# Graph attention on one core: VectorE's operands moved from SBUF to PSUM, part of the one-hot work of the last turns moved to VectorE, and the last stage reordered

## The chip, the cores and the metric

The kernel runs on one core of one Trainium2 chip. What counts is the device time of one execution in microseconds. The engines are written as in the profile: PE is TensorE, DVE is VectorE, ACT is ScalarE, POOL is GpSimd, and SP is the queue that issues most plain DMAs.

## The reference, cut to what matters

One layer of graph attention with 6250 nodes and 206250 edges that are sorted by their target node (6250 of them are loops from a node to itself), 8 heads of 16 columns, and a residual:

```python
h = relu(layernorm(x))
xm = h @ W_n2m.T; xl = xm @ Wl.T + bl; xr = xm @ Wr.T + br
e = ea_f @ We.T                       # ea_f: edge attributes, and their mean per node for a loop
u = leaky_relu(xl[src_f] + xr[dst_f] + e, 0.2)
logits = einsum('ehd,hd->eh', u, att)
mx = segment_max(logits, dst_f); p = exp(logits - mx[dst_f])
alpha = p / segment_sum(p, dst_f)[dst_f]
out = segment_sum(xl[src_f] * alpha, dst_f) + bias
return x + out @ W_m2n.T
```

`leaky_relu(z, 0.2)` is the larger of z and 0.2 z, which is also 0.2 z + relu(0.8 z).

## The kernel before

There are three stages: a prologue (to about 119 us of the trace), the edge loop (to about 2261 us), and the finale.

**Prologue.** It computes xl for all nodes into a table in HBM (`xl_table`), xr into SBUF, and the tables and masks that drive the loop.

**Edge loop.** The edges are cut in 806 pieces of 256, and 427 steps (`STEPS`) take two pieces each. POOL does nothing in this stage but gather the rows of xl for the pieces: 1612 indirect DMAs of 128 rows (line 807; L813 is its wait for the last landings), whose descriptors it writes itself, into a ring `xl_g` of 64 pieces. The engines run their lists in order of turns k, and in one turn they work on different steps. PE makes z of step k in a PSUM bank (`z_ps`, two banks): xr by a one-hot matrix (L828), the attributes (L832), and the transposed copy `xl_z` of the gathered rows (L836). ACT copies the gathered rows to `xl_z` (L906) two turns ahead, and before that waits until the gathers of that step have been issued and landed. ACT then copies z from PSUM to `uT` in SBUF (L939), and DVE makes the leaky relu of `uT` in place (L1027), with both of its inputs in SBUF. PE turns u into logits (L868) and 17 turns later (`LAG`) adds the weighted messages by a one-hot matrix (L882, with `onehot` made by ACT at L928 and L933 and `msg` made by DVE at L1018 and L1023); DVE adds the sums to `acc` (L983, L1006). Once in 8 steps (`BATCH`) come the pieces that find running maxima: two scans over 256 columns (L1037, L1043) into `forth` and `run_max`, a matmul that takes their ends (L849), two scans on one partition (L1051, L1054), then L1067, L1071, L1075 and L1076 on DVE, and transposes (L892, L893). The loop is rolled with a body of 48 turns; turns before 31 and behind the last round are written out. Past the last step (k from 427 on) 19 turns are left in which only the late work is done.

**Finale.** It walks 49 windows of nodes in 7 groups of 7 (b is a group). DVE adds xl to z of the loop edges (L1365), ACT makes the relu part (L1268), DVE joins both (L1370), multiplies, reduces, and finds the falls; ACT makes `weights` by Exp (L1272); DVE makes totals, shares, `old` (L1356) and `own` (L1358); PE transposes and adds them (L1220, L1222) and multiplies by the output matrix (L1235), ACT copies the result (L1294), and POOL adds it to `out` by an accumulating DMA (L1177). `xl_in` (two buffers) is loaded by SP once `own` of an earlier group is done, and `means` (L1318) is made a group ahead in the same loop.

## Time and profile before

| what | value |
|---|---|
| median of 3 runs | 2349.64 us (2345.63 to 2352.04) |
| the profiled execution | 2349.71 us |
| its span, first to last instruction | 2347.9 us |
| outside the span | 1.8 us |
| mean granted TensorE clock | 0.956 of full speed |

The span is what the trace shows, with all its times counted from its first instruction. Busy times of an engine are those of its instructions; an instruction that waits at the head of its engine's queue isn't counted.

### The profile page before, as it was taken

How to read it: one execution, taken by the hardware profiler on the slowest of the kernel's cores; microseconds unless marked ns; L12 is line 12 of the kernel's file. 1: busy time of each engine (PE TensorE's matmuls, PEld its weight loads, DVE VectorE, ACT ScalarE, POOL GpSimd, SP SyncE). 2: the span in 40 equal slices, each digit the busy share in tenths (PEclk: the TensorE clock that was granted, in tenths of full speed). 3: DMA queues.
4: the chain of work that ended last, by engine and by line, in shares of the span. 5: the costliest groups of instructions: out<-in, count | busy, mean ns of one | idle time of the engine just before them, and what ended most of it. 6: DMA issues, size and time to landing. Idle time of an engine off the chain costs nothing. (4 is left out here: it accounts for less than half of the span.)

```text
span 2347.9 us, 62160 instructions
## 1 busy us (share of the span) xinstructions
PE 2203.8 (94%) x11747; PEld 1371.5 (58%) x11748; DVE 1439.1 (61%) x4181; ACT 1550.3 (66%) x4329; POOL 1664.9 (71%) x1813
## 2 busy tenths in 40 slices
PE   3968999999999999999999999999999999999966
PEld 2723566655666566556656665666566656666655
DVE  5723566665666566656666666665666656666677
ACT  2613677676776677667767776777677767777753
POOL 3877777777777777777777777777777777777201
PEclk9956999999999999999999999999999999999989
DMA  5233444444444444444444444444444444444218
GB/s 170 78 86 89 114 116 122 112 110 115 122 115 114 116 119 117 114 116 116 117 114 118 113 118 114 117 114 116 114 121 112 116 112 120 113 116 114 57 54 135
DMA packets 317116, 263.56 MB, mean 112 GB/s; under 512 B 173619, under 2 KB 289637, under 8 KB 316438
## 3 DMA queue, kind: packets, MB, share of 16 engines
q1 hardware_dynamic: 254222, 142.33, 23.8%
q0 software_dynamic: 57632, 113.02, 20.8%
q10 hardware_dynamic: 4840, 3.68, 0.5%
q8 instruction: 131, 2.15, 0.4%
q14 instruction: 291, 2.38, 0.4%
HBM read 247.39 MB, written 16.89 MB: 113 GB/s over the span
## 5 line engine op out<-in xcount | busy, mean ns | idle before, releaser
L807 POOL DMA_INDIRECT xl_g<-xl_table,src_tab x1612 | 1581.0, 981 | 493.6 <-issue 469.5
L1027 DVE SCALAR_TENSOR_TENSOR uT<-uT 128x512 f32<-128x512 f32 x427 | 296.7, 695 | 695.9 <-ACT uT L939 684.6
L882 PE MATMUL banks<-msg,onehot 128*128 128x177 f32 x3416 | 645.7, 332 | 20.0 <-DVE acc L1006 15.1
L882 PEld LDWEIGHTS banks<-msg,onehot 128*128 128x128 f32 x3416 | 530.5, 194 | 185.5 <-issue 149.7
L906 ACT ACTIVATE xl_z<-xl_g 128x256 f32 x854 | 308.9, 408 | 426.7 <-DMA xl_g<-xl_table,src_tab 391.0
L928 ACT ACTIVATE distance<-iota_n,minus_slot 128x128 f32<-128x128 f32 x1708 | 539.1, 386 | 0.0
L832 PE MATMUL banks<-attrT,Wc 32*128 32x512 f32 x854 | 497.7, 663 | 0.0
L828 PE MATMUL banks<-onehotT,xr_parts 128*128 128x256 bf16 x2562 | 366.7, 282 | 30.1 <-issue 22.3
L836 PEld LDWEIGHTS banks<-ident,xl_z 128*128 128x128 f32 x1708 | 184.5, 144 | 349.5 <-issue 263.8
L1018 DVE TENSOR_TENSOR msg<-xl_g,banks 128x256 f32<-128x256 f32 x854 | 320.6, 416 | 75.0 <-PE banks L882 55.3
L939 ACT ACTIVATE uT<-banks 128x512 f32<-128x512 f32 x427 | 251.5, 589 | 123.4 <-PE banks L836 114.9
L828 PEld LDWEIGHTS banks<-onehotT,xr_parts 128*128 x2562 | 250.2, 100 | 88.7 <-issue 43.0
L836 PE MATMUL banks<-ident,xl_z 128*128 128x128 f32 x1708 | 289.2, 293 | 10.6 <-ACT xl_z L906 10.6
L933 ACT ACTIVATE onehot<-distance 128x512 f32<-128x512 f32 x427 | 269.0, 630 | 40.1 <-PE banks L882 2.8
L868 PE MATMUL banks<-uT,att_pad 128*64 128x256 f32 x1708 | 289.5, 419 | 5.7 <-DVE uT L1027 5.1
L832 PEld LDWEIGHTS banks<-attrT,Wc 32*128 32x128 f32 x854 | 129.2, 189 | 94.6 <-issue 93.5
L983 DVE TENSOR_TENSOR acc<-acc,banks 128x177 f32 x427 | 143.3, 335 | 55.8 <-issue 41.7
L993 DVE TENSOR_SCALAR onehotT<-slot_bc,node_of 128x512 bf16<-128x512 bf16 x427 | 151.0, 354 | 2.6 <-DMA slot_bc<-slot_dram 1.8
L1006 DVE TENSOR_TENSOR acc<-acc,banks 128x177 f32 x427 | 142.0, 333 | 4.5 <-issue 1.4
L868 PEld LDWEIGHTS banks<-uT,att_pad 128*64 128x64 f32 x1708 | 86.6, 138 | 90.1 <-issue 76.3
L942 ACT ACTIVATE msg<-rbf 128x128 f32<-128x128 f32 x427 | 129.1, 302 | 0.0
L1023 DVE COPY msg<-banks 128x64 f32<-128x64 f32 x427 | 95.8, 224 | 0.0
(199 smaller groups left out, 1378.1 us busy)
## 6 DMA issues: line engine op xcount, KB each, us to landing
slot_bc<-slot_dram SPq DMA_DIRECT2D x427, 128.0 KB
attrT<-in_attr_cols SPq DMA_DIRECT2D x854, 32.0 KB
rbf<-in_attr_rows SPq DMA_DIRECT2D x854, 32.0 KB
xl_g<-xl_table,src_tab POOLq DMA_INDIRECT x1612
masks<-masks_dram SPq DMA_DIRECT2D x108, 96.5 KB
out<-in_x SPq DMA_DIRECT2D x16, 336.0 KB
out<-result POOLq DMA_DIRECT2D x6, 896.0 KB, 9.7
xl_table<-lr_sb SPq DMA_DIRECT2D x49, 64.0 KB, 1.5
```

What stands on the lines that cost most here:

```text
L807: pool.indirect_dma_start(out=xl_g[:, g % PRING, i], out_offset=None, in_=xl_table, in_offset=bass.IndirectOffsetOnAxis(ap=src_tab[:, j:j ...
L828: nc.tensor.matmul(z[:, h * PIECE:(h + 1) * PIECE], parts_of(xr_parts, w[h], part), onehotT[:, n4, h * PIECE:(h + 1) * PIECE], start=h == ...
L832: nc.tensor.matmul(z, Wc[0:D_RBF], attrT[:, s % TRING], start=False, stop=False)
L836: mm = nc.tensor.matmul(z[:, h * PIECE + i:(h + 1) * PIECE:PT], xl_z[:, s % ZRING, h, i], ident[:], start=False, stop=h == SPLIT - 1 and i ...
L868: mm = nc.tensor.matmul(LT_ps[par][h * ROWS:(h + 1) * ROWS], att_pad[:, ROWS - HEADS - i * HEADS:2 * ROWS - HEADS - i * HEADS], uT[:, n, h ...
L882: mm = nc.tensor.matmul(U_ps[j % 2][:, h], onehot[:, j % 2, t], msg[:, j % 2, t], start=i == 0, stop=i == PT - 1)
L906: nc.scalar.activation(xl_z[:, (s + 2) % ZRING, h].rearrange("p i d -> p (i d)"), xl_g[:, one(pieces[h] & (PRING - 1))].rearrange("p a i d ...
L928: nc.scalar.activation(distance[:, t], iota_n[:], ACT.Abs, bias=minus_slot[:, one(TILES * (k - LAG + 1) + t)]).then_inc(dist_ready, 1)
L933: nc.scalar.activation(onehot[:, m % 2], distance[:], ACT.Relu, scale=-1.0, bias=1.0).then_inc(oh_ready, TICK)
L939: nc.scalar.activation(uT[:, s % 2], z_ps[s % 2], ACT.Copy).then_inc(z_copied, 1)
L1018: nc.vector.tensor_tensor(to[:, two, :, 0:D_HEAD], xl_g[:, one(pieces[h] & (PRING - 1))].rearrange("p a i (h d) -> p (a i) h d", d=D_HEAD) ...
L1027: nc.vector.scalar_tensor_tensor(out=z, in0=z, scalar=SLOPE, in1=z, op0=ALU.mult, op1=ALU.max).then_inc(u_ready, 1)
```

## The change

**In the edge loop**: ACT writes relu(0.8 z) to `uT` in place of a copy of z, and DVE forms 0.2 z + `uT` with z read from the PSUM bank. PE waits for `u_ready` in place of `z_copied` before it writes a z bank again. The two long scans and L1067 write `run_ps`, the unused half of the logits' PSUM bank, and the later ones read it there; a copy of two columns (`run_ends`) serves the matmul at L849. `seq_forth` lies in PSUM. `low` has a buffer of its own, and the wait for `wT_done` moves from the first scan to the second raise.

**Past the last step** (`drained(k)`): ACT makes two of the four one-hot tiles of a turn (two `distance`, one Relu over 256 columns), DVE the two others by one comparison each, behind its `msg` work.

**In the finale**: `xl_in` holds all 7 groups and is loaded without waits. All means are made before the loop, in three instructions, and are turned and copied in five lots. The leaky relu is one DVE instruction behind z (0.2 z against z, by max), without ACT. The shares, `old` and `own` of group n - 1 come behind the falls of group n. `own` is made by POOL for the groups 0 to 5, behind `shares_done`, and POOL issues the result DMA of b - 1 behind `own` of b. PE adds means and parts of group b + 3 before it waits for `gatT` of b.

```diff
-        forth = sb("forth", [P, PIECE])
+        run_ends = sb("run_ends", [P, 2])
         run_max = sb("run_max", [P, PIECE])
-        low, last_max = forth, run_max
+        low = sb("low", [P, PIECE])
+        last_max = run_max
...
-        seq_forth = sb("seq_forth", [1, HEADS * SEQ])
...
+        run_ps = [banks[:, 3 + 3 * par, PIECE:2 * PIECE] for par in (0, 1)]
...
+        seq_forth = banks[0:1, 7, 0:HEADS * SEQ]
```

```diff
                     z = z_ps[s % 2]
                     pe.wait_ge(ohT_ready, k + 1)
                     if inside(k - 2, STEPS):
-                        pe.wait_ge(z_copied, k - 1)
+                        pe.wait_ge(u_ready, k - 1)
...
-                    for i, column in enumerate((run_max[:, 0:1], run_max[:, PIECE - 1:PIECE], masks[:, at_m, 0:1],
+                    for i, column in enumerate((run_ends[:, 0:1], run_ends[:, 1:2], masks[:, at_m, 0:1],
...
-                    for t in range(TILES):
+                    mine = PT if drained(k) else TILES
+                    for t in range(mine):
                         nc.scalar.activation(distance[:, t], iota_n[:], ACT.Abs,
-                                             bias=minus_slot[:, one(TILES * (k - LAG + 1) + t)]).then_inc(dist_ready, 1)
+                                             bias=minus_slot[:, one(TILES * (k - LAG + 1) + t)]
+                                             ).then_inc(dist_ready, TILES // mine)
...
-                    nc.scalar.activation(onehot[:, m % 2], distance[:], ACT.Relu, scale=-1.0, bias=1.0
-                                         ).then_inc(oh_ready, TICK)
+                    nc.scalar.activation(onehot[:, m % 2, 0:mine], distance[:, 0:mine], ACT.Relu, scale=-1.0, bias=1.0
+                                         ).then_inc(oh_ready, TICK - (TILES - mine) // PT)
...
-                    nc.scalar.activation(uT[:, s % 2], z_ps[s % 2], ACT.Copy).then_inc(z_copied, 1)
+                    nc.scalar.activation(uT[:, s % 2], z_ps[s % 2], ACT.Relu, scale=1.0 - SLOPE
+                                         ).then_inc(relu_ready, 1)
```

```diff
+                    if drained(k):
+                        at_t = TILES * (k - LAG + 1) + PT
+                        for t in range(PT, TILES):
+                            oh = nc.vector.tensor_scalar(onehot[:, m % 2, t], iota_n[:],
+                                                         minus_slot[:, at_t + t - PT:at_t + t - PT + 1], 0.0, ALU.add,
+                                                         ALU.is_equal)
+                        oh.then_inc(oh_ready, 1)
                 if inside(k, STEPS):
-                    dve.wait_ge(z_copied, k + 1)
-                    z = uT[:, s % 2]
-                    nc.vector.scalar_tensor_tensor(out=z, in0=z, scalar=SLOPE, in1=z, op0=ALU.mult, op1=ALU.max
-                                                   ).then_inc(u_ready, 1)
+                    dve.wait_ge(relu_ready, k + 1)
+                    nc.vector.scalar_tensor_tensor(out=uT[:, s % 2], in0=z_ps[s % 2], scalar=SLOPE, in1=uT[:, s % 2],
+                                                   op0=ALU.mult, op1=ALU.add).then_inc(u_ready, 1)
...
-                    if inside(b - 1, BATCHES):
-                        dve.wait_ge(wT_done, b)
-                    nc.vector.tensor_tensor_scan(forth[:], masks[:, at_m, 0:PIECE], LT_ps[par], -BIG, ALU.add, ALU.max
-                                                 ).then_inc(forth_done, 1)
+                    nc.vector.tensor_tensor_scan(run_ps[par], masks[:, at_m, 0:PIECE], LT_ps[par], -BIG, ALU.add,
+                                                 ALU.max).then_inc(forth_done, 1)
...
-                    nc.vector.tensor_tensor_scan(run_max[:, ::-1], masks[:, at_m, PIECE:0:-1], forth[:, ::-1], -BIG,
-                                                 ALU.add, ALU.max).then_inc(run_done, 1)
+                    nc.vector.tensor_tensor_scan(run_ps[par][:, ::-1], masks[:, at_m, PIECE:0:-1], run_ps[par][:, ::-1],
+                                                 -BIG, ALU.add, ALU.max).then_inc(run_found, 1)
+                    dve.wait_ge(run_found, b + 1)
+                    nc.vector.tensor_copy(run_ends[:], run_ps[par][:, ::PIECE - 1]).then_inc(run_done, 1)
...
-                    nc.vector.tensor_tensor_scan(seq_forth[:], seq_cut[:, 0:HEADS * SEQ], seq_in[:], -BIG, ALU.add,
...
+                    nc.vector.tensor_tensor_scan(seq_forth, seq_cut[:, 0:HEADS * SEQ], seq_in[:], -BIG, ALU.add,
...
-                    nc.vector.scalar_tensor_tensor(out=forth[:], in0=masks[:, at_m, FIRST:FIRST + PIECE],
-                                                   scalar=ends[:, 0:1], in1=run_max[:], op0=ALU.add, op1=ALU.max
+                    nc.vector.scalar_tensor_tensor(out=run_ps[par], in0=masks[:, at_m, FIRST:FIRST + PIECE],
+                                                   scalar=ends[:, 0:1], in1=run_ps[par], op0=ALU.add, op1=ALU.max
                                                    ).then_inc(firsts_raised, 1)
                     dve.wait_ge(firsts_raised, b + 1)
+                    if inside(b - 1, BATCHES):
+                        dve.wait_ge(wT_done, b)
                     nc.vector.scalar_tensor_tensor(out=run_max[:], in0=masks[:, at_m, LAST:LAST + PIECE],
-                                                   scalar=ends[:, 1:2], in1=forth[:], op0=ALU.add, op1=ALU.max
+                                                   scalar=ends[:, 1:2], in1=run_ps[par], op0=ALU.add, op1=ALU.max
                                                    ).then_inc(run_ready, 1)
```

The finale, cut to its core:

```diff
-        xl_in = sb("xl_in", [P, 2, FB, D_MSG])
+        xl_in = sb("xl_in", [P, FBATCH, FB, D_MSG])
         deg = sb("deg", [P, WINDOWS])
         inv_deg = sb("inv_deg", [P, WINDOWS])
-        mean = sb("mean", [P, 2, 2 * TILES, D_RBF])
-        meanT = sb("meanT", [P, 2, 2, P])
+        mean = sb("mean", [P, FBATCH, 2 * TILES, D_RBF])
+        meanT = sb("meanT", [P, FBATCH, 2, P])
...
-        relu_z = sb("relu_z", [P, FB, D_MSG])
...
             for b in range(2, FBATCH):
-                sp.wait_ge(own_done, b - 1)
-                sp.dma_start(xl_in[:, b % 2], rows(xl_table, b)).then_inc(xl_loaded[b % 2], 16)
+                sp.dma_start(xl_in[:, b], rows(xl_table, b)).then_inc(xl_loaded[b], 16)
...
+            for b in range(LAST_B):
+                pool.wait_ge(shares_done, b + 1)
+                if b >= 2:
+                    pool.wait_ge(gatT_done, b - 1)
+                pool.wait_ge(xl_loaded[b], 16)
+                nc.gpsimd.tensor_tensor(own[:, b % 2].rearrange("p w (h d) -> p w h d", h=HEADS),
+                                        xl_in[:, b].rearrange("p w (h d) -> p w h d", h=HEADS),
+                                        shares[:, b % 2, 1].unsqueeze(3).broadcast_to([P, FB, HEADS, D_HEAD]), ALU.mult
+                                        ).then_inc(own_done, 1)
+                if b:
+                    join(b - 1)
+            join(LAST_B - 1)
...
             turn_means(0)
+            turn_means(1)
             pe.wait_ge(w4_ready, TILES)
             add_means(0)
-            turn_means(1)
-            add_parts(1)
-            add_means(1)
+            for t in range(2, len(turns)):
+                turn_means(t)
+            for n in (1, 2):
+                add_parts(n)
+                add_means(n)
...
+                if b + 3 < FBATCH:
+                    add_parts(b + 3)
+                    add_means(b + 3)
...
+                pe.wait_ge(last_own, half + 1)
...
+                weights_of(b + 1)
...
+            def means(lo, hi):
                 nc.vector.tensor_tensor(
-                    mean[:, n % 2, 0:FB], of(n)[:, :, CNT:AGG],
-                    inv_deg[:, n * FB:(n + 1) * FB].unsqueeze(2).broadcast_to([P, FB, D_RBF]), ALU.mult
-                    ).then_inc(mean_done, 1)
+                    mean[:, lo:hi, 0:FB], acc[:, lo * FB:hi * FB, CNT:AGG].rearrange("p (b w) k -> p b w k", w=FB),
+                    inv_deg[:, lo * FB:hi * FB].rearrange("p (b w) -> p b w", w=FB).unsqueeze(3).broadcast_to(
+                        [P, hi - lo, FB, D_RBF]), ALU.mult).then_inc(mean_done, 1)
...
+            means(2, FBATCH)
+            for n in range(FBATCH + 1):
+                b = n - 1
...
-                    nc.vector.tensor_tensor(z[:], z_ps[:, 0:FB], xl_in[:, n % 2], ALU.add).then_inc(z_added, 1)
-                if n >= 1 and n + 1 < FBATCH:
-                    means(n + 1)
-                if n < FBATCH:
-                    dve.wait_ge(relu_done, n + 1)
-                    nc.vector.scalar_tensor_tensor(out=u[:], in0=z[:], scalar=SLOPE, in1=relu_z[:],
-                                                   op0=ALU.mult, op1=ALU.add).then_inc(u_done, 1)
+                    nc.vector.tensor_tensor(z[:], z_ps[:, 0:FB], xl_in[:, n], ALU.add).then_inc(z_added, 1)
+                    dve.wait_ge(z_added, n + 1)
+                    nc.vector.scalar_tensor_tensor(out=u[:], in0=z[:], scalar=SLOPE, in1=z[:], op0=ALU.mult, op1=ALU.max
+                                                   ).then_inc(u_done, 1)
...
+                if b >= 0:
+                    share = shares[:, b % 2]
+                    dve.wait_ge(weights_done, b + 1)
+                    nc.vector.tensor_tensor(total_old[:], sums_of(b)[:, :, :, D_HEAD], weights[:, b % 2, 0], ALU.mult
...
+                    if b >= 2:
+                        dve.wait_ge(own_done, b - 1)
+                    nc.vector.tensor_tensor(share, weights[:, b % 2],
+                                            inv_total[:].unsqueeze(1).broadcast_to([P, 2, FB, HEADS]), ALU.mult
+                                            ).then_inc(shares_done, 1)
+                    dve.wait_ge(shares_done, b + 1)
+                    if b >= 2:
+                        dve.wait_ge(gatT_done, b - 1)
+                    for lo, hi in halves if b == LAST_B else ((0, FB),):
+                        nc.vector.tensor_tensor(heads(old[:, b % 2])[:, lo:hi], sums_of(b)[:, lo:hi, :, 0:D_HEAD],
+                                                spread(share[:, 0])[:, lo:hi], ALU.mult).then_inc(old_done, 1)
+                        if b == LAST_B:
+                            nc.vector.tensor_tensor(heads(own[:, b % 2])[:, lo:hi], heads(xl_in[:, b])[:, lo:hi],
+                                                    spread(share[:, 1])[:, lo:hi], ALU.mult).then_inc(last_own, 1)
```

## Rows read from the trace of the kernel before

**Rows 1.** The page: busy time of each engine, its share and its instructions.

```profile
PE 2203.8 (94%) x11747; PEld 1371.5 (58%) x11748; DVE 1439.1 (61%) x4181; ACT 1550.3 (66%) x4329; POOL 1664.9 (71%) x1813
```

**Rows 2.** One source line: duration least/median/most in ns, first and last start.

```profile
L807 POOL DMA_INDIRECT xl_g<-xl_table,src_tab x1612: 940/945/1461, 119.7 to 2190.8; - x180
```

**Rows 3.** Windows, the gathers alone: window, its length, busy time and count.

```profile
119.00:541.30 422.30, 322.92 (x324) 0.86 0.44 108
541.30:2161.70 1620.40, 1235.01 (x1265) 0.98 0.47 116
```

**Rows 4.** Timeline of ACT around the end of the gathers: start, length, what it waited for.

```profile
2192.03 0.72 ACT L906 ACTIVATE xl_z<-xl_g 128x256 f32 x2 [1.72 <-POOLq L813]
...
2211.67 0.60 ACT L939 ACTIVATE uT<-banks 128x512 f32<-128x512 f32 x1 [1.58 <-PE banks L836]
```

**Rows 5.** Timeline: gathers (POOL) beside the DVE instructions that run when they start.

```profile
146.53 0.69 DVE L1027 SCALAR_TENSOR_TENSOR uT<-uT 128x512 f32<-128x512 f32 x1 [22.30 <-ACT uT L939]
146.58 1.46 POOL L807 DMA_INDIRECT xl_g<-xl_table,src_tab  x1 [0.30 <-issue]
...
1053.49 0.68 DVE L1037 TENSOR_TENSOR_SCAN forth<-masks,banks 128x256 f32<-128x256 bf16 x1
1053.54 0.94 POOL L807 DMA_INDIRECT xl_g<-xl_table,src_tab  x1 [0.30 <-issue]
...
2175.14 0.69 DVE L1027 SCALAR_TENSOR_TENSOR uT<-uT 128x512 f32<-128x512 f32 x1 [1.67 <-ACT uT L939]
2175.52 1.12 POOL L807 DMA_INDIRECT xl_g<-xl_table,src_tab  x1 [0.30 <-issue]
```

**Rows 6.** Timeline of ACT: two copies of z, eight steps apart.

```profile
801.73 0.60 ACT L939 ACTIVATE uT<-banks 128x512 f32<-128x512 f32 x1 [0.57 <-PE banks L836]
...
838.86 0.60 ACT L939 ACTIVATE uT<-banks 128x512 f32<-128x512 f32 x1 [0.56 <-PE banks L836]
```

**Rows 7.** Windows: the z copies alone, their time and count.

```profile
541.30:2161.70 1620.40, 198.57 (x336) 0.98 0.47 116
```

**Rows 8.** Timeline of PE at the edge of a loop round.

```profile
768.06 1.46 PE L828 MATMUL banks<-onehotT,xr_parts 128*128 128x256 bf16 x6 [3.17 <-issue]
```

**Rows 9.** Window behind that edge: busy time of each engine, granted clock, DMA.

```profile
768.00:775.00 7.00, 6.94 (x21) 3.72 (x22) 3.25 (x10) 4.34 (x12) 5.37 (x6) 0.51 0.50 111
```

**Rows 10.** Timeline of ACT in two turns past the last step.

```profile
2254.84 1.26 ACT L928 ACTIVATE distance<-iota_n,minus_slot 128x128 f32<-128x128 f32 x4
...
2256.92 0.39 ACT L928 ACTIVATE distance<-iota_n,minus_slot 128x128 f32<-128x128 f32 x1
```

**Rows 11.** Window from one turn's first message product to the next turn's.

```profile
2254.28:2256.70 2.42, 1.44 (x8) 1.20 (x8) 1.51 (x5) 2.34 (x7) 0.00 (x0) 1.00 0.00 0
```

**Rows 12.** Group of one line: count, busy us and mean ns.

```profile
L633 DVE TENSOR_SCALAR far_row<-far_sign 1x128 f32<-1x128 f32 x1 | 0.2, 215 | 0.1
```

**Rows 13.** Timeline of DVE over one turn of the last stage.

```profile
2305.76 1.08 DVE L1365 TENSOR_TENSOR z_loop<-banks,xl_in 128x896 f32<-128x896 f32 x1
...
2307.86 1.09 DVE L1370 SCALAR_TENSOR_TENSOR u_loop<-z_loop,relu_z 128x896 f32<-128x896 f32 x1 [0.72 <-ACT relu_z L1268]
...
2312.19 0.25 DVE L1341 TENSOR_TENSOR total_old<-acc,weights 128x56 f32<-128x56 f32 x1 [0.36 <-ACT weights L1272]
...
2315.58 1.08 DVE L1365 TENSOR_TENSOR z_loop<-banks,xl_in 128x896 f32<-128x896 f32 x1
```

**Rows 14.** Groups of POOL: elementwise work of two widths.

```profile
L384 POOL TENSOR_TENSOR xr_parts<-rest,xr_parts 128x128 f32 x40 | 17.7, 443 | 0.0
...
L374 POOL CAST slots<-keys 128x512 bf16<-128x512 f32 x3 | 1.7, 601 | 0.0
```

**Rows 15.** Timeline: POOL and DVE both reading SBUF.

```profile
92.46 0.42 POOL L384 TENSOR_TENSOR xr_parts<-rest,xr_parts 128x128 f32 x1
92.47 0.57 DVE L648 TENSOR_TENSOR rest<-lr_sb,xr_parts 128x128 f32<-128x128 f32 x1
```

**Rows 16.** Timeline of PE in the last stage: the output products of one group.

```profile
2308.86 3.21 PE L1235 MATMUL banks<-W_outT,gatT 128*128 128x256 f32 x14
```

136 lines of the change are left out of this document (50 added, 86 removed).

## The prediction

> **What bounds the kernel now.** I read the page first, then the gathers' line, windows, the timeline. On the page PE looks like the bound, with 94% [rows 1], and POOL is busy 71% of the time. That is misleading: POOL's gathers follow one another without a pause from 119.7 to 2190.8 us [rows 2]. The only idle time between two of them is 0.30 us, which ends with nothing awaited [rows 5]: it is POOL's own overhead. So the period is 2071.1 us / 1611 = 1.286 us, of which 0.945 (the median) and 0.305 are fixed. What is left, 1.286 - 1.250 = 0.036 us each or 58 us in all, is gathers longer than the median. ACT waits for the last of them until 2192.0, and the last z copy comes 20 us later [rows 4]. Whatever POOL loses shows up in the loop's end, as long as PE doesn't set the pace itself.
>
> Which gathers are long? Beside the two whose start falls in an L1027 (DVE, both inputs in SBUF) one sees 1.46 and 1.12 us; beside the scan L1037, whose second input is in PSUM, 0.94 [rows 5]. In the first pair L1027 ends 0.64 us into the gather and the gather is 0.51 too long; in the last it ends 0.31 in and the excess is 0.18. So the gather reaches a point 0.13 us in, where it waits until DVE has finished. I went through all 268 gathers over 0.96 us (excess 58.7 us; the outer pairs of [rows 5] are the first and last of L1027's 160). By the DVE instruction whose end fits: L1027 38.2 us, L1054 8.5 (47), L1043 6.9 (16), L1067 0.3, all of which the change takes to PSUM; L993 1.7 (25), a memset of `acc` 1.6, L1051 1.2, which stay. It removes 53.9 us of delay.
>
> PE's own pace: eight steps take 37.13 us where PE isn't starved [rows 6]. At each edge of a loop round PE stands still for 3.17 us [rows 8] and then works for 7 us at a granted clock of 0.51, the 1.2 GHz level [rows 9], which costs half of its 6.94 busy us again: 6.6 us an edge.
>
> **The edge loop.** *To 541.3 us*: 324 gathers took 322.9 us [rows 3], 16.7 over the median's rate. Nothing is in store yet and PE has fewer matmuls at first, so all of it counts. 15.2 of it is of the four lines above; I let 1.5 return, since instructions fall elsewhere: -13.7 us. *From 541.3 to 2161.7*: 1265 gathers [rows 3] for 336 steps [rows 7] in 1620.4 us. Without delays the gathers need 1265 x 1.250 = 1581, with what stays (3 us) or three times more than that in new coincidences 1584 to 1593. PE needs 42 x 37.13 + 7 x 6.6 = 1606. PE takes over as the bound, and only 14.5 us of the 40 are gained. *Behind that* four gathers' time is left and PE runs at its own pace already: 0. The loop: -28 us. Bounds: if PE's edges overlap with less than I count, up to -36; if new coincidences bring back half of the removed delay, -20.
>
> Costed at nothing in the loop: L939 as Relu (same shape, same engine); L1027 with one input in PSUM (DVE is idle 39% of the span [rows 1], and L1037 beside its SBUF twin L1043 shows that PSUM costs nothing that is seen; 0.1 us more a step would lie in that idle time too); PE's wait for `u_ready` of two steps ago, which L868 of that step has already waited for in the turn before. The copy `run_ends` adds some 0.15 us on DVE before L849, but PE comes to L849 only behind the z matmuls, about 2 us later. If that cover were gone it would cost 54 x 0.15 = 8 us. Writes of DVE to PSUM aren't in the trace; from nothing to 0.1 us on six instructions in 8 steps, hidden likewise.
>
> **Past the last step.** 16 turns make one-hot tiles. A turn without batch work lasts 2.08 us and is ACT's [rows 10]: its distances, its Relu and the copy of attributes. It falls to about 1.3. DVE works 1.51 us in such a turn [rows 11], 1.65 with the short gaps. A comparison over 128 columns costs 0.215 us alone [rows 12], some 0.2 in a row; with two DVE comes to 2.05. So the turn changes hands and not its length. In the eight turns that already hang on DVE's batch pieces the 0.4 is added, in part. Bounds -1 and +3; I take +1, as an estimate.
>
> **The finale.** A turn lasts 2315.58 - 2305.76 = 9.82 us, all DVE's chain [rows 13]. Out of it come: `own` (1.0; the same width as L1370's 1.09, overlapped), the hop to ACT for relu with the means in it (2.10 from z to u becomes 1.10), and the wait for `weights` (0.36 idle, 0.4 with its ends). That is 2.45 us; 7.4 are left, six times: -14.7. Against it: `own` on POOL. A POOL instruction costs 0.443 for 128 columns with two inputs, and 0.601 for 512 with one [rows 14]. Bounds for 896: 1.08, as on DVE, and 7 x 0.443 = 3.1; with 0.19 of fixed cost, which the two POOL rows fit, 1.9. It starts when `old` starts on DVE, both read SBUF twice, and one of them waits: when POOL was 0.01 us ahead, DVE took 0.57 us for what takes 0.28 [rows 15]. Here DVE follows its own semaphore and should win; POOL then runs from the end of `old`, under z (input in PSUM), and holds up u by 1.9 - 1.1 = 0.85 us, five times: +4.3. At the end PE must make the output products of group 5 (3.2 us [rows 16]) before it turns the last group, which waited for DVE before: +3.2. The long means instruction up front, 1 us, is mostly under POOL's set-up: +0.5. The finale: -6.7, say -6. Bounds: -11 (no contention) and +1 (POOL 3.1 us and ahead each time). The `xl_in` loads win nothing: the chain of waits names one of them, but DVE's turns keep their 9.82 us through it.
>
> **The sum** is made against the profiled execution, 2349.71 us (span 2347.9 and 1.8 around it), which is the median's 2349.64 within 0.1: 2349.7 - 28 + 1 - 6 = 2316.7; I say 2316.
>
> **A rule that speaks against it.** The trace has L1027 lengthen gathers. The Trainium skill ("SBUF — State Buffer", section "Who interferes with whom") holds that a tensor-tensor instruction takes only the shared pair's read interface and that descriptor generation needs the write interface, so that it doesn't stall such DMAs. By that rule the loop would gain nothing.
>
> **Rivals.**
> 1. *POOL isn't relieved*: the delay follows DVE's timing, not its operands. Then 2349.7 + 1 - 6 = 2345. Against it: [rows 5], and L1037, which covered that point of 13 gathers without one exceeding 0.948. Chance 0.06. The rule above belongs here.
> 2. *Delays move*: half of the 54 us returns by L993, L1051 and others, and POOL stays the bound in stretches: the loop gains 20 or less, 2325 to 2335. For it: phases are locked to the gathers; against: what stays costs 5 us now. 0.14.
> 3. *The finale gains nothing or loses* (POOL ahead at `own`): 2322 to 2324. 0.12.
> 4. *Slower*: L993, which stays in SBUF, falls on the sensitive point in every step. At 0.354 us it can delay at most 0.354 - 0.13 - 0.06 = 0.17 a step, 427 x 0.17 = 72 us; from 0.126 us a step on it eats the 54. At worst 2349.7 + 18 - 5 = 2363. Today it costs 1.7 us in all. 0.03.
> 5. *As summed*: 2304 to 2322. 0.65.
>
> The range 2303 to 2330 holds case 5, case 3 and half of case 2. 0.3% is 7 us, about what a measurement can tell. Faster by more: cases 2, 3, 5 and a little of 1, 0.92; within: 0.05; slower: 0.03.
>
> **What would show it.** Gathers over 0.96 us: under a hundred, none beside L1027's successor. POOL begins to wait for DVE (`msg_ready`) between gathers. ACT's waits for gathers nearly vanish behind 541 us, and eight steps take 37.1 us there. Turns of the finale: about 8.2 us, with a gap of 0.85 before u. Drain turns 2.05 us with DVE full. I'd be wrong if eight steps took over 37.5 without a wait for gathers (PSUM reads or writes cost more), or if the gathers' excess stayed.

## The result and the profile after

The changed kernel took 2314.86 us (median of 4 runs, 2312.69 to 2320.73), the kernel before, run beside it, 2350.84 (4 runs, 2345.63 to 2355.26). The ratio is 0.9852, with a 95% interval from 0.9823 to 0.988. 2316 was predicted, with a range of 2303 to 2330.

The profiled execution of the changed kernel is the slowest of its four, 2320.73 us with a span of 2318.9. Against the profiled one of before (2349.71) it is 29.0 us shorter. The table splits both spans in four stages at the same events. "Loop" ends with the start of the last copy or relu of z on ACT, "drain" with the last addition to `acc`, "last stage" with the end of the last `result` on DVE, and "behind" is the output DMAs.

| stage, us | before | changed | difference | predicted |
|---|---|---|---|---|
| loop (with the prologue) | 2211.7 | 2186.5 | -25.2 | -28 |
| drain | 49.9 | 54.0 | +4.0 | +1 |
| last stage | 80.4 | 69.8 | -10.6 | -6 |
| behind | 5.9 | 8.6 | +2.7 | 0 |
| span | 2347.9 | 2318.9 | -29.0 | -33 |

The page: busy time of each engine (the counterpart of [rows 1]), the source line of the gathers ([rows 2]) with what ended POOL's idle time before them and who waited for them:

```profile
PE 2194.0 (95%) x11747; PEld 1366.3 (59%) x11748; DVE 1457.0 (63%) x4257; ACT 1552.1 (67%) x4288; POOL 1636.4 (71%) x1819
```

```profile
L813 POOL DMA_INDIRECT xl_g<-xl_table,src_tab x1612: 940/944/1642, 120.0 to 2147.3; - x180
...
  issue: 477.5, 1559
  DVE msg L1027: 10.1, 33
  DVE msg L1032: 6.1, 20
...
  ACT xl_z L912: 164.7, 158
```

The busy shares have hardly moved. What has moved is the start of the last gather, 2190.8 to 2147.3. The period is (2147.3 - 120.0) / 1611 = 1.258 us. Of the 58 us over 0.945 + 0.305 of before, 14 are left. Counted over all 1612, 120 gathers last over 0.96 us, where there were 268.

A gather that starts just behind an L1042 (u, now with z from PSUM) and one beside a memset of `acc`, in a timeline (the counterpart of [rows 5]):

```profile
163.85 0.69 DVE L1042 SCALAR_TENSOR_TENSOR uT<-banks,uT 128x512 f32<-128x512 f32 x1 [3.56 <-ACT uT L947]
163.91 0.94 POOL L813 DMA_INDIRECT xl_g<-xl_table,src_tab  x1 [0.30 <-issue]
...
164.75 1.09 DVE L978 MEMSET acc<- 128x1239 f32 x1 [0.21 <-issue]
165.16 1.63 POOL L813 DMA_INDIRECT xl_g<-xl_table,src_tab  x1 [0.30 <-issue]
```

The first pair stands as the first pair of [rows 5] does, to within 0.01 us, and the gather takes 0.94 us in place of 1.46. The second pair is one of six memsets that now delay a gather by 0.7 us each.

Counted over both traces, the order of the starts matters as well as the operand. In the kernel before, 157 L1027 start at least 0.05 us ahead of a gather and end more than 0.16 us into it, and all 157 gathers are longer than 0.96 us. In the changed kernel 173 L1042 stand like that, and none of the gathers is longer. Of the 47 L1027 of before that start later, up to 0.13 us behind the gather's start, only one makes it longer, though they run over the point 0.13 us in; 31 of them are longer themselves, 0.70 to 0.76 us in place of 0.69. This is one of the others, in the trace of before:

```profile
1048.48 0.94 POOL L807 DMA_INDIRECT xl_g<-xl_table,src_tab  x1 [0.30 <-issue]
1048.60 0.69 DVE L1027 SCALAR_TENSOR_TENSOR uT<-uT 128x512 f32<-128x512 f32 x1 [2.13 <-ACT uT L939]
```

Two relus of z eight steps apart on ACT ([rows 6]), the start of a round on PE ([rows 8]), and the window behind it with the busy times of PE, PEld, DVE, ACT and POOL, then granted clock, DMA share and GB/s ([rows 9]):

```profile
805.75 0.60 ACT L947 ACTIVATE uT<-banks 128x512 f32<-128x512 f32 x1
...
842.87 0.60 ACT L947 ACTIVATE uT<-banks 128x512 f32<-128x512 f32 x1
```

```profile
757.75 1.10 PE L834 MATMUL banks<-onehotT,xr_parts 128*128 128x256 bf16 x6 [3.73 <-issue]
```

```profile
757.70:764.70 7.00, 6.95 (x22) 3.92 (x23) 3.27 (x10) 3.92 (x11) 5.42 (x6) 0.54 0.46 114
```

Eight steps take 37.12 us, nearly everywhere behind step 31 except across the edge of a round. A window with the gathers alone and one with the z relus alone, from step 79 to eleven steps before the end ([rows 3, 7]):

```profile
531.30:2136.30 1605.00, 1215.40 (x1279) 0.98 0.49 117
```

```profile
531.30:2136.30 1605.00, 199.80 (x336) 0.98 0.49 117
```

These are the 336 steps of [rows 7], now in 1605.0 us and not 1620.4; "PE needs 1606" was the forecast.

The drain: a window from the last relu of z to the last addition (PE, PEld, DVE, ACT, POOL busy, then the clock), and DVE over a turn without batch work:

```profile
2186.50:2240.50 54.00, 40.59 (x184) 33.16 (x184) 41.91 (x147) 24.64 (x78) 0.00 (x0) 0.81 0.07 17
```

```profile
2233.55 0.76 DVE L1027 TENSOR_TENSOR msg<-xl_g,banks 128x256 f32<-128x256 f32 x2 [0.45 <-PE banks L888]
...
2234.36 0.47 DVE L1036 TENSOR_SCALAR onehot<-iota_n,minus_slot 128x128 f32<-128x128 f32 x2
...
2235.48 0.75 DVE L1027 TENSOR_TENSOR msg<-xl_g,banks 128x256 f32<-128x256 f32 x2
```

The turn lasts 1.93 us with DVE full. Over the whole drain DVE is busy 41.9 us.

A turn of the last stage on DVE with POOL's `own` beside it ([rows 13]):

```profile
2279.93 1.09 DVE L1395 TENSOR_TENSOR old<-acc,shares 128x896 f32<-128x896 f32 x1
2279.99 2.61 POOL L1201 TENSOR_TENSOR own<-xl_in,shares 128x896 f32<-128x896 f32 x1 [1.24 <-DVE shares L1388]
2280.94 1.08 DVE L1360 TENSOR_TENSOR z_loop<-banks,xl_in 128x896 f32<-128x896 f32 x1
2282.06 1.48 DVE L1362 SCALAR_TENSOR_TENSOR u_loop<-z_loop 128x896 f32<-128x896 f32 x1
...
2288.73 1.08 DVE L1360 TENSOR_TENSOR z_loop<-banks,xl_in 128x896 f32<-128x896 f32 x1
```

The turn takes 7.79 us where it took 9.82. `own` shows 2.61 us, of which it spends 1.03 until `old` ends, so its own time is 1.6, if it stands still until then; no run shows that by itself. u takes 1.48 in place of 1.09, because `own` still runs. The Trainium skill ("SBUF — State Buffer", section "Who interferes with whom") says that a DVE instruction with two SBUF inputs contends with a GpSimd instruction that reads SBUF; this row agrees with it.

The end, in a timeline:

```profile
2305.52 1.63 POOL L1193 DMA_DIRECT2D out<-result  x1 [5.77 <-ACT result L1311]
...
2308.15 2.15 DVE L1405 TENSOR_TENSOR result<-banks,x_in 128x1024 f32<-128x1024 f32 x2 [6.55 <-PE banks L1283]
2309.40 0.38 SPq L1172 DMA_DIRECT2D out<-result  x1
2310.33 0.67 SPq L1174 DMA_DIRECT2D out<-result  x1
2311.05 1.23 SPq L1176 DMA_DIRECT2D out<-result  x1
```

DVE waits 6.55 us for PE ahead of its last result, where it waited 4.42. POOL issues the accumulating DMA of group 5 only 3.9 us before SP issues the first part of group 6 (7.4 us in the kernel before), and SP's last issue takes 1.23 us in place of 0.55. The DMA packets in the trace say what the plain DMAs wait for: the first packet of SP's queue moves 3.6 us after its issue, 1.3 us ahead of the end of POOL's last accumulating packet. In the kernel before it moves 0.9 us after its issue, 0.1 us behind that end.

### The profile page after: what moved, and what is told of

Read it like the earlier page. It is cut to its first block and busy times, and to the rows that moved or that the text cites. A ratio compares the mean times of both kernels' runs of the same rounds, so it can differ in the third digit from the quotient of the medians.

```text
span 2318.9 us, 62219 instructions
## 1 busy us (share of the span) xinstructions
PE 2194.0 (95%) x11747; PEld 1366.3 (59%) x11748; DVE 1457.0 (63%) x4257; ACT 1552.1 (67%) x4288; POOL 1636.4 (71%) x1819
## 5 line engine op out<-in xcount | busy, mean ns | idle before, releaser
L813 POOL DMA_INDIRECT xl_g<-xl_table,src_tab x1612 | 1537.1, 954 | 493.6 <-issue 477.5
L1042 DVE SCALAR_TENSOR_TENSOR uT<-banks,uT 128x512 f32<-128x512 f32 x427 | 294.9, 691 | 613.8 <-ACT uT L947 600.1
L935 ACT ACTIVATE distance<-iota_n,minus_slot 128x128 f32<-128x128 f32 x1676 | 529.8, 386 | 6.9 <-DVE onehot L1036 6.9
L1027 DVE TENSOR_TENSOR msg<-xl_g,banks 128x256 f32<-128x256 f32 x854 | 320.6, 416 | 99.9 <-PE banks L888 73.6
L941 ACT ACTIVATE onehot<-distance 128x512 f32<-128x512 f32 (+1 forms) x427 | 265.5, 622 | 39.6 <-PE banks L888 2.4
L1002 DVE TENSOR_SCALAR onehotT<-slot_bc,node_of 128x512 bf16<-128x512 bf16 x427 | 157.3, 368 | 1.8 <-DMA slot_bc<-slot_dram 1.8
```

The costliest lines, as they stand in the source:

```text
L813: pool.indirect_dma_start(out=xl_g[:, g % PRING, i], out_offset=None, in_=xl_table, in_offset=bass.IndirectOffsetOnAxis(ap=src_tab[:, j:j ...
L935: nc.scalar.activation(distance[:, t], iota_n[:], ACT.Abs, bias=minus_slot[:, one(TILES * (k - LAG + 1) + t)]).then_inc(dist_ready, TILES ...
L941: nc.scalar.activation(onehot[:, m % 2, 0:mine], distance[:, 0:mine], ACT.Relu, scale=-1.0, bias=1.0).then_inc(oh_ready, TICK - (TILES - m ...
L1027: nc.vector.tensor_tensor(to[:, two, :, 0:D_HEAD], xl_g[:, one(pieces[h] & (PRING - 1))].rearrange("p a i (h d) -> p (a i) h d", d=D_HEAD) ...
L1042: nc.vector.scalar_tensor_tensor(out=uT[:, s % 2], in0=z_ps[s % 2], scalar=SLOPE, in1=uT[:, s % 2], op0=ALU.mult, op1=ALU.add).then_inc(u_ ...
```

## The experiments

All of these kernels, and a control, differ from their base by one more register operation per step on ACT and one per wait of POOL for free ring places:

```diff
-                    pool.wait_ge(msg_ready, freed[g // FREED % FREE_ROW])
+                    pool.wait_ge(msg_ready, freed[g // FREED % FREE_ROW] & 2047)
...
-                    act.wait_ge(landed, pieces[SPLIT - 1] * PT + (PT + FLIGHT))
+                    act.wait_ge(landed, (pieces[SPLIT - 1] & 1023) * PT + (PT + FLIGHT))
```

> Control for all experiments: the changed kernel with one more register operation per step on ACT (the piece number that the wait for the landings uses is cut to 10 bits, which changes no value) and one per wait of POOL on freed ring places. All other experiments have them too. It should give the time of the changed kernel, 2313 to 2321 us, with the last z copy near 2186 us in the trace, 54 us from there to the last addition to acc, and 70 us from there to the last result on DVE. If the added register operations cost anything, the eight-step pace of 37.1 us rises.

It measured 2314.90 us, ratio 0.9854 (0.9832 to 0.9877), so the added operations cost nothing that shows. The table has all kernels, each with its ratio to the kernel before on its own chip and the stages of its profiled execution. "Excess" is how much the gathers over 0.96 us are above 0.945 us, all together.

| kernel | median us | ratio (95%) | excess | loop | drain | last stage | behind |
|---|---|---|---|---|---|---|---|
| before | 2350.84 | | 58.7 | 2211.7 | 49.9 | 80.4 | 5.9 |
| changed | 2314.86 | 0.9852 (0.9823 to 0.988) | 15.7 | 2186.5 | 54.0 | 69.8 | 8.6 |
| changed, control | 2314.90 | 0.9854 (0.9832 to 0.9877) | 16.7 | 2182.0 | 51.7 | 70.8 | 8.6 |
| 1, u alone | 2326.21 | 0.9902 (0.9881 to 0.9923) | 23.2 | 2186.5 | 47.3 | 80.3 | 6.0 |
| 2, maxima alone | 2341.72 | 0.9963 (0.9947 to 0.9978) | 51.6 | 2203.4 | 48.0 | 82.5 | 5.9 |
| 3, last stage alone | 2343.15 | 0.997 (0.9961 to 0.998) | 59.0 | 2210.8 | 50.2 | 70.9 | 8.5 |
| 4, tiles on ACT | 2312.83 | 0.9845 (0.9828 to 0.9861) | 15.4 | 2182.5 | 49.7 | 70.3 | 8.6 |
| 5, extra, SBUF | 2370.02 | 1.0084 (1.0068 to 1.0101) | 84.7 | 2239.0 | 52.3 | 69.7 | 8.7 |
| 6, extra, PSUM | 2347.88 | 0.9989 (0.9974 to 1.0003) | 6.8 | 2209.7 | 55.6 | 69.7 | 8.6 |
| 7, two parts | 2296.29 | 0.9773 (0.9755 to 0.979) | 10.0 | 2161.7 | 52.9 | 69.7 | 8.6 |
| 8, own on DVE | 2318.12 | 0.9857 (0.9842 to 0.9872) | 16.4 | 2184.6 | 52.1 | 72.2 | 8.6 |
| 9, reordered end | 2316.01 | 0.9849 (0.9836 to 0.9862) | 15.1 | 2183.2 | 51.3 | 70.0 | 10.4 |
| 10, group 5 plain | 2310.13 | 0.9817 (0.98 to 0.9833) | 14.3 | 2181.6 | 48.4 | 70.2 | 6.1 |
| 11, and own 5 on DVE | 2308.06 | 0.9805 (0.979 to 0.982) | 14.4 | 2180.4 | 49.7 | 69.6 | 6.1 |

**1. The leaky relu alone.**

```diff
-                    nc.scalar.activation(uT[:, s % 2], z_ps[s % 2], ACT.Copy).then_inc(z_copied, 1)
+                    nc.scalar.activation(uT[:, s % 2], z_ps[s % 2], ACT.Relu, scale=1.0 - SLOPE
+                                         ).then_inc(z_copied, 1)
...
-                    z = uT[:, s % 2]
-                    nc.vector.scalar_tensor_tensor(out=z, in0=z, scalar=SLOPE, in1=z, op0=ALU.mult, op1=ALU.max
+                    nc.vector.scalar_tensor_tensor(out=uT[:, s % 2], in0=z_ps[s % 2], scalar=SLOPE, in1=uT[:, s % 2],
+                                                   op0=ALU.mult, op1=ALU.add
```

> The kernel before, with only the leaky relu changed: ACT writes relu(0.8 z), DVE reads z from PSUM. Theory A (a gather is held up by a DVE instruction with two SBUF inputs): the gathers lose the 38.2 us put down to L1027, excess over the median from 57.7 to 19 to 24 us; PE becomes the loop's bound at about step 31 as in the changed kernel, so the loop's end (last z copy, 2211.7 before) comes 20 to 25 us earlier, nearly all that the whole change gives there; about 2327 us. Rival B (the delay follows DVE's timing and not its operands): excess stays near 58 us and the time near 2350. Rival C (each edit pays in proportion to its delay): the loop gains 38.2/53.9 of 25 us, 18 us, 2332 us.

The source line of the gathers:

```profile
L807 POOL DMA_INDIRECT xl_g<-xl_table,src_tab x1612: 940/944/1646, 119.3 to 2154.2; - x180
```

The last gather starts 36.6 us earlier than before (38.2 was L1027's part), and the loop ends at 2186.5, where the profiled execution of the changed kernel has it too. Theory A holds, the rivals fall. The one edit gives nearly the whole gain of the loop, since PE takes over; experiment 7 shows that.

**2. The running maxima alone**: the two long scans and the first raise write and read `run_ps`, and `seq_forth` lies in PSUM, as in the diff of the change; u is as before:

```diff
-                        pe.wait_ge(u_ready, k - 1)
+                        pe.wait_ge(relu_ready, k - 1)
...
-                    nc.scalar.activation(uT[:, s % 2], z_ps[s % 2], ACT.Relu, scale=1.0 - SLOPE
-                                         ).then_inc(relu_ready, 1)
+                    nc.scalar.activation(uT[:, s % 2], z_ps[s % 2], ACT.Copy).then_inc(relu_ready, 1)
```

> The kernel before, with only the running maxima moved to PSUM (the two long scans, the first raise, the scan on one partition), u as before in SBUF, one-hot tiles and last stage as before. Theory A: the gathers lose about the 15.7 us put down to L1043, L1054 and L1067, excess near 42 us, POOL stays the bound and the loop ends 13 to 16 us earlier: about 2336. If new coincidences take it back, 2345 or more.

It took 2341.72 us, where about 2336 was expected. The excess falls by 7.1 us and not by 15.7, and the loop ends 8.3 us earlier and not 13 to 16. The u instruction delays more than it did (45.4 us by the same attribution, 38.2 before). So the predicted "delays move" is seen in this one trace, while a long instruction with two SBUF inputs remains. Beside experiment 1 this edit adds little: in the first round behind step 31 (48 steps) the changed kernel takes 227.5 us, its control 228.0 and experiment 1 231.7, so some 4 us, and in the full rounds behind that all three take 228 to 231. The last stage of this kernel is that of before and yet 2.1 us longer in its trace: DVE waits 3.3 us for PE ahead of the first z, and not 1.2. So one or two us between the stages of two single traces prove nothing by themselves.

**3. The last stage alone**, put into the kernel before: the part of the diff that is headed by the finale, and nothing of the loop.

> The kernel before, with only the new last stage. From the last addition to acc to the end of the last result on DVE: 80.4 us before, 69.8 in the changed kernel; behind that 5.9 us of output DMA before, 8.6 after. So -10.6 + 2.7 = -8 us, 2342 us, if the three parts are independent. If the output DMA's 2.7 us are chance of one run, 2339.

Measured -9.5 and +2.6 us by the stages, 2343.15 against 2350.23 for the kernel before in that set, -7.1. The last stage doesn't depend on the loop, and its output DMAs end 8.5 us behind the last result here too, so this isn't chance.

**4. The one-hot tiles past the last step back on ACT.**

```diff
         def drained(k):
-            return isinstance(k, int) and k >= STEPS
+            return False
```

> The changed kernel, with ACT making all four one-hot tiles past the last step as before. Loop and last stage as in the changed kernel. From the last z copy to the last addition to acc: 54.0 and 51.7 us in the two traces of the changed kernel, 49.9, 47.3, 48.0 and 50.2 in the four traces where ACT makes all tiles. If DVE's two comparisons are what lengthens it (DVE is the full engine there), it falls to 47 to 50.5 us and the time to 2310 to 2313; if the longer stretch is only the lower granted clock of that run, it stays above 51.

The window of its drain, and that of the kernel before:

```profile
2182.50:2232.10 49.60, 35.42 (x184) 28.60 (x182) 36.10 (x115) 35.95 (x110) 0.00 (x0) 0.93 0.08 19
```

```profile
2211.70:2261.60 49.90, 36.68 (x184) 30.10 (x183) 35.67 (x113) 35.97 (x110) 0.00 (x0) 0.90 0.08 18
```

The comparisons are 6.2 us of DVE (41.9 against 35.7) and save 11.3 us of ACT (36.0 against 24.6), but the drain gets no shorter. The control has the same granted clock as the kernel before, 0.90, and its drain is 1.8 us longer. The changed kernel has 0.81 and 4.0 us; its PE does the same 184 matmul entries in 40.6 us, and not 36.7. The turns say it more sharply: of the turns with batch work, five are 0.4 us longer in the control than in this experiment (twice 3.24 against 3.63, twice 3.77 against 4.17, 2.96 against 3.34), 2.0 us in all, as much as the two drains differ by. By the medians the difference is 2.1 us, inside the intervals of the two kernels; the turns are the better evidence. In the six traces with tiles on DVE (changed, control, 5 to 8) the drain takes 51.7 to 55.6 us, 53.1 on average; in the eight with all of them on ACT (before, 1 to 4, 9 to 11) 47.3 to 51.3, 49.3 on average.

**5 and 6. One more DVE instruction per step, with both inputs in SBUF, and its twin with one in PSUM.**

```diff
+                    nc.vector.tensor_tensor(uT[:, s % 2], uT[:, s % 2], uT[:, s % 2], ALU.max).then_inc(pad_done, 1)
+                    dve.wait_ge(pad_done, k + 1)
```

```diff
+                    nc.vector.tensor_tensor(uT[:, s % 2], z_ps[s % 2], uT[:, s % 2], ALU.add).then_inc(pad_done, 1)
+                    dve.wait_ge(pad_done, k + 1)
-                    nc.vector.scalar_tensor_tensor(out=uT[:, s % 2], in0=z_ps[s % 2], scalar=SLOPE, in1=uT[:, s % 2],
+                    nc.vector.scalar_tensor_tensor(out=uT[:, s % 2], in0=z_ps[s % 2], scalar=SLOPE - 1.0, in1=uT[:, s % 2],
```

> The changed kernel, with one more DVE instruction a step ahead of u: a tensor-tensor max of uT with itself, 128x512, both inputs in SBUF; u waits for it. The values don't change. Theory A (two SBUF inputs hold up a gather, for any such instruction): the gathers' excess rises by 30 to 50 us, from 16 to 46 to 66, the last gather starts near 2185 us, POOL bounds the loop again and the last z copy comes near 2206, about 2335 in all. Rival B (a tensor-tensor instruction takes only the read interface and doesn't hold up descriptors): excess stays at 14 to 20 us, and the time is that of the twin with its input in PSUM.

> The twin: the extra tensor-tensor instruction, same shape, adds z from PSUM to uT, and u subtracts 0.8 z in place of adding 0.2 z (the same value, rounded otherwise). Both theories: excess 14 to 20 us as in the changed kernel. It shows what 0.6 to 0.7 us more DVE work ahead of u costs by itself: nothing (2315) if u has that much slack before the logits' matmul, up to 427 x 0.6 us if it hasn't.

Experiment 5, timeline and the gathers' group (busy, mean ns, idle):

```profile
165.43 0.69 DVE L1043 TENSOR_TENSOR uT<-uT 128x512 f32<-128x512 f32 x1 [3.55 <-ACT uT L948]
165.48 1.45 POOL L814 DMA_INDIRECT xl_g<-xl_table,src_tab  x1 [0.30 <-issue]
```

```profile
L814 POOL DMA_INDIRECT xl_g<-xl_table,src_tab x1612 | 1606.4, 997 | 493.8 <-issue 475.8
```

Experiment 6, the same:

```profile
161.04 0.69 DVE L1043 TENSOR_TENSOR uT<-banks,uT 128x512 f32<-128x512 f32 x1 [2.30 <-ACT uT L948]
161.10 0.94 POOL L814 DMA_INDIRECT xl_g<-xl_table,src_tab  x1 [0.30 <-issue]
```

```profile
L814 POOL DMA_INDIRECT xl_g<-xl_table,src_tab x1612 | 1528.3, 948 | 493.6 <-issue 478.4
```

Both instructions last 0.69 us and start 0.05 to 0.06 us before the gather; one makes it 1.45 us, the other leaves 0.94. Over all gathers it is (997 - 948) x 1612 = 79 us. Of the added instructions that start at least 0.05 us ahead of a gather and still run 0.16 us into it, 191 of 191 make it longer in experiment 5, and none of 184 in experiment 6. The place of the operand decides, for a plain tensor-tensor instruction as well (one takes the max, the other adds, but they last equally long). The Trainium skill ("SBUF — State Buffer", section "Who interferes with whom") infers that tensor-tensor instructions leave descriptor generation alone, because they take only the read interface. For the gathers the time doesn't come out by that rule, and the measurement decides. The rule itself may still hold, since another DMA that POOL issues isn't held up. In the trace of the kernel before:

```profile
2313.57 1.09 DVE L1356 TENSOR_TENSOR old<-acc,shares 128x896 f32<-128x896 f32 x1
2314.07 1.65 POOL L1177 DMA_DIRECT2D out<-result  x1 [7.41 <-ACT result L1294]
```

`old` has two SBUF inputs and runs until 0.59 us into the issue of the accumulating DMA, which takes 1.65 us; with no DVE instruction beside it, in the changed kernel at 2305.52, it takes 1.63. What the gather has in addition is a read of its row numbers, from `src_tab` in SBUF. That this read is what waits is likely and not shown: no run takes it away.

I had expected 30 to 50 us more excess and about 2335 us. It became 69 more than in the changed kernel and 2370.02 us. Behind the added instruction lie 58 of the 84.7 us, in 199 gathers: in the first steps 15 of 16 hit, later fewer than half. And 33 us of the time aren't delay at all, as the twin shows.

The twin has a cost of its own. The prediction took 0.1 us more on DVE as free, which no run tests; 0.7 us more ahead of u, with the gathers at their fastest, gives 2348 us, 33 more than the changed kernel. Eight steps take 37.5 us and not 37.1, the loop ends 23 to 28 us later and the drain is longer. Part of these 0.7 us has no cover; which instruction waits for u first wasn't traced further.

**7. Less work for PE**: the loop's one-hot product takes two of the three parts of xr, so that the least significant part is missing from the result.

```diff
-                        for part in range(PARTS):
+                        for part in range(PARTS - 1):
                             nc.tensor.matmul(z[:, h * PIECE:(h + 1) * PIECE], parts_of(xr_parts, w[h], part),
```

> The changed kernel, with PE making only two of the three bf16 parts of xr by the one-hot matrix in the loop (two of six matmuls of 0.28 us left out per step; the least significant part of xr is missing from the result). If PE is what bounds the loop from step 31 on, the pace falls below 37.1 us in eight steps until POOL's gathers, which ended 38 us before the last z copy and need 20 behind the last one, take over: the last z copy 15 to 20 us earlier, 2296 to 2301 in all, ACT's waits for gathers back. If POOL still bounds it, no change.

Who waited for the gathers, in the source line's answer, and ACT in a stretch where POOL sets the pace:

```profile
  ACT xl_z L912: 428.8, 292
```

```profile
707.00 0.72 ACT L912 ACTIVATE xl_z<-xl_g 128x256 f32 x2 [1.57 <-DMA xl_g<-xl_table,src_tab]
```

2296.29 us, 18.6 less; the loop ends 20 to 25 us earlier, and ACT waits for gathers in 292 places where it waited in 158. So PE bounds the changed kernel's loop. POOL is the next bound: the 336 steps behind step 79 now take 1583 us and not 1605, and the prediction's rate without delays, 1265 x 1.250, gives 1581. The last z relu had been expected 15 to 20 us earlier.

**8. `own` on DVE in all groups.**

```diff
-                nc.gpsimd.tensor_tensor(own[:, b % 2].rearrange("p w (h d) -> p w h d", h=HEADS),
...
-                        if b == LAST_B:
-                            nc.vector.tensor_tensor(heads(own[:, b % 2])[:, lo:hi], heads(xl_in[:, b])[:, lo:hi],
+                        nc.vector.tensor_tensor(heads(own[:, b % 2])[:, lo:hi], heads(xl_in[:, b])[:, lo:hi],
```

> The changed kernel, with DVE making own for all seven groups, behind old, and POOL left with the result DMAs. In the changed kernel a group takes 7.39 us of DVE where own doesn't hold up u and 7.78 where it does (u 1.48 in place of 1.09). With 1.0 more on DVE and no hold-up it should take 8.4 us: 7.39 + 1.0. The last stage then takes 0.6 x 5 = 3 us longer than the 70 us of the changed kernel, less what comes back behind the last group, where PE waits for POOL's own of group 5 until 1.7 us behind old: 72 to 73 us; 2317. If POOL's own cost more than it saved, the stage would get shorter than 70.

A turn takes 2288.17 - 2279.78 = 8.39 us and the last stage 72.2, both as expected; 2318.12. POOL's `own` is worth 1.4 us against the control's stage, 2.4 against the changed kernel's; the turns, 8.39 against 7.39 and 7.78, are the firmer evidence.

**9. A reordered end** (tiles on ACT, `own` of group 5 on DVE, PE turns the last group ahead of the products of group 5).

```diff
                 pe.wait_ge(gatT_ready, b + 1)
+                if b == LAST_B - 1:
+                    turn_last()
                 for half, (lo, hi) in enumerate(halves):
...
+                if b == LAST_B - 2:
+                    weights_of(b + 2)
+                if b == LAST_B - 1:
+                    for half, (lo, hi) in enumerate(halves):
+                        act.wait_ge(gatT_done, FBATCH + half)
+                        nc.scalar.activation(last_gatT[:, lo:hi], T_ps[:, lo:hi], ACT.Identity, bias=bias_col[:]
+                                             ).then_inc(gatT_ready, 1)
```

> A version that should beat both: the changed kernel with ACT making all four one-hot tiles past the last step (2.1 us faster by the run that has only this), and the end of the last stage reordered. DVE makes own of group 5 (it idled 1.06 us there), ACT makes the last Exp ahead of the result of group 4, PE turns the last group ahead of the output products of group 5, and the turned last group has a buffer of its own. Behind the last product of group 5 the wait of 0.4 us, the transposes of 0.9 us and half of the gatT copy go, and PE starts group 5 some 0.6 us earlier: last stage 70.3 to about 68.5 us, 2311. If the output DMAs set the end (8.6 us behind the last result), the gain is given back there: 2312.8.

This one missed its forecast: 2316.01 us, a last stage of 70.0 where 68.5 was expected, and 10.4 us behind the last result. Of the 3.9 us that its trace is longer than that of experiment 4, 2.4 lie in the loop and the drain, which the edit doesn't touch. Its end in a timeline shows why the end came late:

```profile
2301.43 1.63 POOL L1195 DMA_DIRECT2D out<-result  x1 [7.07 <-ACT result L1330]
2302.36 2.15 DVE L1419 TENSOR_TENSOR result<-banks,x_in 128x1024 f32<-128x1024 f32 x2 [6.24 <-PE banks L1294]
```

The end of the span (2314.9) lies 11.84 us behind the end of POOL's issue of group 5, 2303.06. In the eight other traces with the new last stage it is 11.6 to 11.9, whatever stands between. With the old last stage it is 12.6, and 5.9 to 6.0 behind the last result. So in the new stage the accumulating DMA of group 5 sets the end, by holding back the plain ones behind it, and this reorder had put it later against the rest: POOL's issue ends 68.5 us behind the last addition, in experiment 4 67.2.

**10 and 11. Group 5 written by plain DMAs**, with x added on DVE, and in 11 its `own` on DVE and the last Exp ahead of the result of group 4.

```diff
+            for half, (lo, hi) in enumerate(halves):
+                dve.wait_ge(y_done, 2 * (LAST_B - 1) + half + 1)
+                nc.vector.tensor_tensor(result[:, (LAST_B - 1) % 2, lo:hi], y_ps[:, lo:hi], x_fifth[:, lo:hi], ALU.add
+                                        ).then_inc(fifth_ready, 1)
...
-            join(LAST_B - 1)
```

> The changed kernel with ACT making all one-hot tiles past the last step, and the output of group 5 written like that of group 6: DVE adds x to it (it idled 6.5 us there) and SP writes it by plain DMAs; ACT's result copy and POOL's accumulating DMA of group 5 go. Theory A (in the new last stage the accumulating DMA of group 5 sets the end: in the nine traces with it the end comes 11.6 to 11.9 us behind the end of POOL's issue, while it stands 8.5 to 10.4 us behind the last result): the end comes 5.5 to 7 us behind the last result in place of 8.6, 2309.5 to 2311 where the kernel without this edit took 2312.8. Rival B (the end follows the last result by the amount of bytes alone): 8.6 us stay, 2312.8.

> The same, and DVE makes own of group 5, and ACT makes the last Exp ahead of the result of group 4. DVE no longer waits 1.06 us for weights and PE turns group 5 about 0.6 us earlier; since the chain from there (transposes, gatT, output products of group 5, the last group's) is PE's, the last result comes 0.6 us earlier than in the run without: about 2309.5. If POOL's hold-up of u and the wait were hidden anyway, no difference that is seen.

The end of 11, in a timeline:

```profile
2297.58 2.15 DVE L1428 TENSOR_TENSOR result<-banks,x_in 128x1024 f32<-128x1024 f32 x2 [2.79 <-PE banks L1295]
2298.83 0.37 SPq L1179 DMA_DIRECT2D out<-result  x1
2299.76 0.37 SPq L1181 DMA_DIRECT2D out<-result  x1
2300.18 0.57 SPq L1183 DMA_DIRECT2D out<-result  x1
```

The end stands 6.1 us behind the last result in both, and SP's last issue is back at 0.57 us. Theory A holds. 10 is 2310.13 us, 11 is 2308.06 with the last stage 0.6 us shorter as expected; between the two the medians can't tell. Version 11 takes 1.95% less than the kernel before (1.8 to 2.1%) and about 0.5% less than the changed kernel, each by its ratio to before.

## Why the prediction was right, and where its terms were off

**The mechanism** was right. The delay that was removed comes from DVE instructions with two SBUF inputs, and goes with the operand ([rows 5], experiments 1, 5 and 6). Rival 1 is out; the 2345 us that it gave are 30 off. Rivals 3 and 4 didn't come: the last stage gained, and the comparisons of L993's kind cost 3.7 us of delay. The reading that a gather waits at a point 0.13 us in is half of the rule: it gives the length of the delay, but only an instruction that started 0.05 us or more before the gather delays it (157 of 157, against 1 of 47).

**"To 541.3 us: -13.7"** was -10.1 (the relu of step 79 starts at 531.3, before at 541.4). Two things were missed. The memsets of `acc` went from 1.6 to 4.7 us of delay, which is rival 2 on a small scale. And PE takes over at step 31, 303.8 us: eight steps take 37.0 to 37.1 from there on. I had POOL as the bound for another 240 us. Some of the 3.6 us is this one execution: in the control the relu of step 79 starts at 529.6, which is -11.8.

**"From 541.3: -14.5", "PE needs 1606"**: 1605.0 us for the same 336 steps, the best term of the sum. 37.13 for eight steps was right, and an edge costs 7.0 us and not 6.6 (rounds take 229.8 us, six times 37.13 is 222.8). Experiment 7 shows PE as the bound. The loop: -25.2, inside -20 to -36 (-29.7 in the control).

**Signs**. POOL doesn't begin to wait for `msg_ready`. The 53 gaps of 0.31 us that bear DVE's name (there were 79 before) are no longer than those that bear none. The ring of 64 pieces takes up the lead: the last gather starts 39 us before the last z relu, and not 21. A faster producer with a deep ring shows as earlier work, not as a wait. "Under a hundred" long gathers were 120, with none behind L1042. ACT's waits for gathers behind 541 us fell from 213 to 58 us and didn't nearly vanish. The turns of the finale took 7.8 us and not 8.2, with u longer in place of a gap before it.

**The drain, +1 (-1 to +3)**: +4.0 in the profiled execution, +3.8 between the averages of all traces with and without it, +1.8 between the two traces with a granted clock of 0.90. The turn without batch work is 1.93 us (2.05 predicted, 2.08 before), so that part was right. What I undersized is the batch turns, where DVE's pieces and comparisons add up: 2.0 us in five of them (experiment 4), which I had counted only in part. That the lower clock follows from PE's waits is argued from the windows alone.

**The last stage, -6 (-11 to +1)**: -10.6. Seven turn starts span 43.6 us and not 58.9; of this, 2.8 come back behind the last turn, where the last group's shares stand, with a wait of 1.06 for `weights`. That is -12.5 where I had -14.7 + 4.3 = -10.4. The mis-sized term is POOL's `own`: 1.6 us and not 1.9, so u is held up by 0.39 in four of the turns and not by 0.85 in five. The products of group 5 cost 2.1 and not 3.2, and the means up front nothing (0.2 us less).

**A term that was missing**: the output DMAs, +2.7. I took the time behind the last result as fixed. The accumulating DMA of group 5 moved nearer to the end and holds back the plain ones behind it; experiments 9 and 10 show that it sets the end.

Sum by the stages: -25.2 + 4.0 - 10.6 + 2.7 = -29.1, so 2320.6 for the profiled execution, which took 2320.73; the forecast for it was 2316.7. The median is 5.9 us lower than this one execution. Of that the control's trace shows 4.5 us in the loop and 2.3 in the drain, and its last stage 0.9 longer. So that the median lies within 1.2 us of 2316 is in good part luck: the terms erred by +3, +3, -5 and +3, +4 in all, and the executions of the changed kernel differ among themselves by 8 us.

## What to carry to other kernels

When an engine's instructions have a sharp common duration, look at the ones that are longer, and at what runs beside them at their start; moving one operand of one instruction to PSUM was worth 1%. Size such a gain by the next bound, not by the sum of the delays: 54 us of delay could go, the loop became 25 us shorter, and the second edit of the same kind added nothing to 4 us to the first. When the end of a kernel is brought forward, ask which DMA is issued before the last ones, because it may hold them back and so set the end.

## What the runs showed of the hardware that I had not expected

- A plain tensor-tensor instruction on DVE with both inputs in SBUF (0.69 us) lengthened a gather's instruction on POOL from 0.94 to 1.45 us; one with an input in PSUM left it at 0.94 (experiments 5 and 6). POOL's issue of an accumulating DMA stayed at 1.65 us beside such an instruction.
- It is a matter of who starts first. L1027 lengthened all 157 gathers that it was at least 0.05 us ahead of and still ran beside at 0.16 us; of 47 that it was not ahead of by as much, one. Instead it was itself up to 0.07 us longer there.
- Two SBUF inputs aren't the only case. A memset of 1.09 us on DVE, without any input, lengthened a gather to 1.63 us, and an onehotT comparison with one SBUF input in bf16 (0.35 us) made some 50 of them longer by 0.07 us on average.
- With an accumulating DMA of 896 KB issued 3.9 us ahead of three plain ones, the queue instruction of the third took 1.23 us and not 0.55, and the end came 2.5 us later (8.6 against 6.1 behind the last result) than with plain DMAs alone. In the last 15 us of the trace the accumulating packets moved at most 195 KB in a us, the plain ones up to 361.
- In the drain the granted clock was 0.81 in one trace and 0.90 in the other of the same instructions, which made PE's busy time 40.6 and 37.0 us.
